# Moving the last block's query products and their copies in an attention and FFN kernel

## The chip, the cores and the metric

The kernel runs on one core of one Trainium2 chip. The metric is the device time of one execution in microseconds, and the time before is the median of three runs. TensorE multiplies, VectorE, ScalarE and GpSimd (POOL in the profile) work on its results, and SyncE (SP) issues most of the transfers.

## What is computed

64 sequences of 32 positions with 512 channels go through a conditioned mixing layer, attention with 32 heads in 8 key groups, a residual, a grouped convolution and a gated FFN with low-rank factors. The part that matters here is the attention; each sequence attends causally to its own 32 positions.

```python
q = jnp.dot(x, Wq).reshape(b, t, H, HD).transpose(0, 2, 1, 3)
kv = jnp.dot(x, Wkv).reshape(b, t, G, 2, HD).transpose(2, 3, 0, 1, 4)
...
scores = jnp.einsum('bhqd,bhkd->bhqk', q, k)
scores = jnp.where(causal[None, None], -jnp.inf, scores)
weights = jax.nn.softmax(scores * (1.0 / HD ** 0.5), axis=-1)
ctx = jnp.einsum('bhqk,bhkd->bhqd', weights, v)
...
x = x + _L0_attn_ref(_L0_cond_ref(...), Wq, Wkv, Wo, bo)
x = x + _L0_ffn_ref(_L0_cond2_ref(...), ...)
```

## The kernel before

The 2048 rows are projected in four blocks of 512 (`BLOCKS`). For each block TensorE makes the mixed input `y`, its value product, its key product and `REP` = 4 query products. A product in `project(blk, j)` (L1147) is 12 matmuls of 128x512: high parts, low parts of `y`, low parts of the weight; j = 0 is the key, j = 1 to 4 are the queries. They alternate between two PSUM banks, `front[0]` and `front[1]`, and ScalarE empties each with `copy_queries` (L728), so that a product waits for the copy of the one two before it. The last block's queries go to `q_odd`, and SyncE stores them by `store_queries` (L444) to be loaded again for the steps that need them.

Attention runs in 16 steps (`QUADS`), each of four sequences, as a software pipeline over the engines. The loop variable is n; each engine has its own loop, written out by hand, and the order in it is the order of the work:

- TensorE (L1248): scores n (L1257 the mask, L1263 the 16 products), then late query products where n is 1 or 2 (`LATE_Q` = 2, so the last two of the four), the grouping of the convolution's weights at n = 2 (L1271), the context of step n - 3 (L1285), the output projection of step n - 4 (L1299).
- VectorE (L982): transpose of scores n (L989), sum of step n - 1 (L997), maxima of step n (L980), reciprocal (L1004), transpose of the probabilities of step n - 2 (L1010), low parts of the context of step n - 3 (L1025).
- GpSimd (L641): shift of step n by its maxima (L646), normalisation of step n - 1 (L653), splits of the down factors at n = 2, 3, 4 (L660, L667), residual addition of step n - 4 (L676). Ahead of the loop it clears `v_wide`, splits the four low parts of the output weight `wo_lo` by a subtraction (L631), and clears four edges of the convolution's windows (L637, L638).
- ScalarE (L801): the late query's copy at n = 1 and 2 (L803), ahead of that step's exponential (L822); spreading of the values in even steps (L791), packing of the convolution's weights at n = 2 (L827), one copy of the down factors in each of the first five steps (L832), which waits for `down_sb`, and the high part of the context of step n - 2 (L842).
- SyncE (L513): loads of query and key groups (`queries_and_keys`, L454; group g serves steps 2g and 2g + 1), the store of the last queries at n = 3, the convolution's shift at n = 4. `down_sb` is loaded right behind the first two groups (L512).

The first two groups' loads start when the last block's key product has been copied to `k_all` (L754, L476). Four of the eight `k_wide` loads of the first group are issued by ScalarE (L769), the others by SyncE. Scores 0 wait for all of them. Scores n wait for the transpose of scores n - 2.

The high parts of the output weight (`wo_hi`, L779) are copied by ScalarE ahead of the attention loop, two behind each of the two early query copies.

Of the kernel before, what the change touches and what calls it, by code (L numbers as in the profile page):

```python
# [18 lines left out]
G, REP, HD = 8, 4, 16  # L19
# [5 lines left out]
BLOCKS = N // BLOCK  # L25
TILES = BLOCK // P
BB = BLOCK // S
BT = P // S
# [17 lines left out]
SUM = 1  # L46
# [4 lines left out]
F2_HEAD = 8  # L51
STAGES = 3
RESID_PHASES = ((), (0, 1), (2, 3), ())
LATE_Q = 2
GROUPS = S // CG
SPOTS = 2 * BT
WIN = D // SPOTS
# [3 lines left out]
def adaln_attention_ffn(nc, x, params, wq, wk, wv, wo, bo, conv, f1, f3, f2, up_factors, down_factors,  # L61
                        ident, causal, out):
    with ExitStack() as ctx:
# [46 lines left out]
        wo_loaded = sem("wo_loaded")  # L110
        wo_hi_split = sem("wo_hi_split")
        wo_lo_split = sem("wo_lo_split")
# [57 lines left out]
        near_zeroed = sem("near_zeroed")  # L170
# [34 lines left out]
        with ExitStack() as room:  # L205
            wo_hi = sb("wo_hi", [GD, REP, D], room, F32R)
# [41 lines left out]
        with ExitStack() as room:  # L248
            f2_hi_head = sb("f2_hi_head", [P, F2_HEAD, D], room, F32R)
            near_head = sb("near_head", [P, 2, BB, WIN], room)  # L250
# [39 lines left out]
        with ExitStack() as room:  # L290
            sb("room6_head", [P, DC * HID], room)
            wo_sb = sb("wo_sb", [GD, REP, D], room)
        with ExitStack() as room:
            sb("room6_head_again", [P, DC * HID], room)
            near_tail = sb("near_tail", [P, 2, BB, WIN], room)
# [39 lines left out]
        def in_windows(columns):  # L335

            return columns.rearrange("p (r w h) -> p h r w", r=BT, h=2)
# [242 lines left out]
        def _(pool):  # L580
# [33 lines left out]
            for i, phase in enumerate(RESID_PHASES):  # L614
                pool.wait_ge(y_lo_ready, (i + 1) * DC)
                for tile in [blk * TILES + t for blk in phase for t in range(TILES)]:
                    blk, t = divmod(tile, TILES)
# [8 lines left out]

            pool.wait_ge(front_filled, (BLOCKS - 1) * USES + DC + 1)
            pool.memset(v_wide[:, :, :, :, :], 0.0).then_inc(v_cleared, 1)
            for j in range(REP):
                pool.wait_ge(wo_hi_split, j + 1)  # L630
                pool.tensor_tensor(wo_lo[:, j, :].rearrange("p (h r w) -> p h r w", h=2, r=BT), in_windows(wo_sb[:, j, :]),  # L631
                                   wo_hi[:, j, :].rearrange("p (h r w) -> p h r w", h=2, r=BT).bitcast(F32),
                                   ALU.subtract).then_inc(wo_lo_split, 1)

            pool.wait_ge(wo_lo_split, REP)
            for pair in (near_head, near_tail):
                pool.memset(pair[:, :, :, 0:1], 0.0).then_inc(near_zeroed, 1)  # L637
                pool.memset(pair[:, :, :, WIN - 1:WIN], 0.0).then_inc(near_zeroed, 1)  # L638
            wide = [P, 2 * BT * REP, S]

            for n in range(QUADS + OUT):  # L641
                if due(n, 0):

                    pool.wait_ge(top_ready, n + 1)
                    pr = probs[:, n % PROBS]
                    pool.tensor_tensor(pr, pr, top[:, n % PROBS].unsqueeze(2).to_broadcast(wide), ALU.subtract)\  # L646
                        .then_inc(shifted, 1)
                if due(n, SUM):

                    m = n - SUM  # L650
                    pool.wait_ge(inv_ready, m + 1)
                    pr = probs[:, m % PROBS]
                    pool.tensor_tensor(pr, pr, inv[:, m % PROBS].unsqueeze(2).to_broadcast(wide), ALU.mult)\  # L653
                        .then_inc(probs_ready, 1)
                if n in (SUM + 1, SUM + 2):

                    own = slice((n - SUM - 1) * HID // 2, (n - SUM) * HID // 2)
                    pool.wait_ge(down_stacked, 1)
                    pool.wait_ge(probs_ready, n - SUM + 1)
                    pool.tensor_tensor(a_down_s[2 * S:3 * S, own], a_down[2 * S:3 * S, own],  # L660
                                       down_part[2 * S:3 * S, own].bitcast(F32), ALU.subtract)\
                        .then_inc(down_lo_stacked, 1)
                    pool.wait_ge(down_lo_stacked, n - SUM)
                if n == SUM + 3:
                    pool.wait_ge(down_stacked, 2)
                    pool.wait_ge(probs_ready, n - SUM + 1)
                    pool.tensor_tensor(b_down_s[S:2 * S, :], b_down[S:2 * S, :],  # L667
                                       down_part[S:2 * S, 0:D].bitcast(F32), ALU.subtract).then_inc(down_lo_stacked, 1)
                    pool.wait_ge(down_lo_stacked, 3)
                if due(n, OUT):  # L670

                    tile = n - OUT
                    t = tile % TILES
                    pool.wait_ge(front_emptied[tile % 2], emptied(PROJECTED + tile) + 1)
                    pool.wait_ge(resid_loaded[t], 16 * (tile // TILES + 1))
                    pool.tensor_tensor(rows[:, t, :], out_stage[:, tile % 2, :], rows[:, t, :], ALU.add)\  # L676
                        .then_inc(x1_ready, 1)
# [7 lines left out]
        def _(act):  # L685
# [42 lines left out]
            def copy_queries(blk, j):  # L728

                n = DC + 2 + j  # L730
                act.wait_ge(front_filled, blk * USES + n + 1)
                act.copy(q_stage[blk % 2][:, :, j, :], front[n % 2][:, :].rearrange("p (b s) -> p b s", s=S))\
                    .then_inc(front_emptied[n % 2], 1)

            for i in range(BLOCKS // 2):
                for half in range(2):
                    blk = 2 * i + half
                    for c in range(DC):

                        act.wait_ge(front_emptied[c % 2], blk * (USES // 2) + emptied(c) + 1)  # L740
                        act.copy(y_hi[:, c, :], y_t[:, c, :]).then_inc(y_hi_ready, 1)
                        if blk == 0:

                            act.wait_ge(wq_loaded, 16)
                            act.copy(wkq_hi[:, 1 + c, :, :], wq_sb[:, :, c, :]).then_inc(wkq_hi_split, 1)
                    n = DC
                    act.wait_ge(front_filled, blk * USES + n + 1)
                    act.copy(v_all[:, blk * TILES:(blk + 1) * TILES, :],
                             front[n % 2][:, :].rearrange("p (t c) -> p t c", t=TILES))\
                        .then_inc(front_emptied[n % 2], 1)  # L750
                    n = DC + 1

                    act.wait_ge(front_filled, blk * USES + n + 1)
                    act.copy(k_all[:, :, blk * 2:(blk + 1) * 2, :].rearrange("p g c s -> p c g s"),  # L754
                             front[n % 2][:, :].rearrange("p (c g s) -> p c g s", c=2, s=S))\
                        .then_inc(front_emptied[n % 2], 1)
                    if blk == 0:
                        spread_mix_act(2)
                        spread_mix_act(3)
                        copy_up_factors(0)  # L760
                    if half == 1:

                        act.wait_ge(q_stored[0], 16 * (i + 1))
                    if blk == BLOCKS - 1:

                        act.wait_ge(front_emptied[n % 2], blk * (USES // 2) + emptied(n) + 1)
                        act.wait_ge(zeros_set, 3)
                        for k in range(HEADS, G):
                            act.dma_start(k_wide[k * HD:(k + 1) * HD, 0, :, k % HEADS, :], k_all[0:HD, k, :, :])\  # L769
                                .then_inc(k_loaded[0], 16)  # L770
                    for j in range(REP - (LATE_Q if blk == BLOCKS - 1 else 0)):
                        copy_queries(blk, j)
                        if blk == 0:
                            copy_up_factors(1 + j)
                        if blk == BLOCKS - 1:

                            act.wait_ge(wo_loaded, 16)
                            for part in range(j * REP // (REP - LATE_Q), (j + 1) * REP // (REP - LATE_Q)):
                                act.copy(wo_hi[:, part, :].rearrange("p (h r w) -> p h r w", h=2, r=BT),  # L779
                                         in_windows(wo_sb[:, part, :])).then_inc(wo_hi_split, 1)  # L780

            copies = stack_copies(a_down, b_down, a_down_s, b_down_s, down_part[2 * S:3 * S, :],
                                  down_part[S:2 * S, 0:D])
# [15 lines left out]
            act.wait_ge(front_emptied[DC % 2], emptied((BLOCKS - 1) * USES + DC) + 1)  # L799
            act.wait_ge(v_cleared, 1)  # L800
            for n in range(QUADS + OUT):  # L801
                if 1 <= n <= LATE_Q:
                    copy_queries(BLOCKS - 1, REP - LATE_Q + n - 1)  # L803
                if due(n, 0) and n % 2 == 0:

                    if n >= 4:
# [13 lines left out]
                if due(n, 0):  # L820
                    act.wait_ge(shifted, n + 1)
                    act.activation(probs[:, n % PROBS], probs[:, n % PROBS], ACT.Exp, scale=SCALE)\  # L822
                        .then_inc(exp_ready, 1)
                if n == LATE_Q:

                    act.wait_ge(conv_grouped, 1)
                    act.copy(conv_sb[:, :, :, :, :], ps[7][:, 0:GROUPS * 2 * S]  # L827
                             .rearrange("p (g h q o) -> p g h q o", g=GROUPS, h=2, q=BT)).then_inc(conv_packed, 1)
# [249 lines left out]
        def _(pe):  # L1078
# [169 lines left out]
            for n in range(QUADS + OUT):  # L1248
                if due(n, 0):
# [15 lines left out]
                                           q_t[part, c, :, :].rearrange("p j s -> p (j s)"),  # L1265
                                           start=False, stop=(b == BT - 1))
                    mm.then_inc(scores_ready, 1)
                if 1 <= n <= LATE_Q:
                    project(BLOCKS - 1, REP - LATE_Q + n)
                if n == LATE_Q:  # L1270
                    group_conv()  # L1271
                if due(n, TURN + 1):
                    m = n - TURN - 1
# [179 lines left out]
```

## Time and profile before

| what | before |
|---|---|
| median of 3 runs | 592.26 us (591.83 to 592.91) |
| the profiled execution | 592.54 us, its span 590.7 us |
| TensorE busy | 578.9 us, 98% |
| VectorE, ScalarE, GpSimd busy | 237.6, 172.2, 182.3 us |
| mean granted TensorE clock | 0.991 |
| projections of the last block, then attention | scores 0 start at 101.87, scores 15 at 183.76 |

Times are microseconds from the start of the span. A timeline row says when a group starts, how long it takes, the engine, the line, the operation, output <- input, and in brackets the engine's idle time ahead of it with what ended it. A row of the chain of waits says when a piece starts, how long it lasts and what it is; the chain is followed back from the last instruction to whatever released it.

### The profile page before, as it was taken

How to read it: one execution, taken by the hardware profiler on the slowest of the kernel's cores; microseconds unless marked ns; L12 is line 12 of the kernel's file. 1: busy time of each engine (PE TensorE's matmuls, PEld its weight loads, DVE VectorE, ACT ScalarE, POOL GpSimd, SP SyncE). 2: the span in 40 equal slices, each digit the busy share in tenths (PEclk: the TensorE clock that was granted, in tenths of full speed). 3: DMA queues.
4: the chain of work that ended last, by engine and by line, in shares of the span. 5: the costliest groups of instructions: out<-in, count | busy, mean ns of one | idle time of the engine just before them, and what ended most of it. 6: DMA issues, size and time to landing. Idle time of an engine off the chain costs nothing.

```text
span 590.7 us, 8111 instructions
## 1 busy us (share of the span) xinstructions
PE 578.9 (98%) x3227; PEld 466.8 (79%) x3227; DVE 237.6 (40%) x340; ACT 172.2 (29%) x296; POOL 182.3 (31%) x132
## 2 busy tenths in 40 slices
PE   9999999799999999999999999999999999999997
PEld 6988988577777778887778888778888777888885
DVE  1434542789999851111641111244111234211112
ACT  3561224564654353332121111121111102211110
POOL 3438463699999595434200000000000000000000
PEclk9999999969999999999999999999999999999999
DMA  7975648545666774000019000007400002200001
GB/s 244 344 306 158 225 161 267 144 102 172 178 157 178 240 220 88 1 0 1 1 71 226 5 1 1 2 1 206 94 0 0 0 0 76 67 0 1 0 1 71
DMA packets 70735, 59.24 MB, mean 100 GB/s; under 512 B 45072, under 2 KB 61840, under 8 KB 69584
## 3 DMA queue, kind: packets, MB, share of 16 engines
q1 hardware_dynamic: 69840, 57.43, 32.2%
q10 hardware_dynamic: 864, 1.38, 0.6%
q8 instruction: 22, 0.36, 0.3%
q14 instruction: 9, 0.07, 0.0%
HBM read 40.94 MB, written 16.79 MB: 98 GB/s over the span
## 4 chain that ended last, share of the span: by engine, by line
PE 84%; POOL 6%; DVE 4%; ACT 2%; SPq 1%; DMA 1%; issue 1%; POOLq 0%; DVEq 0%
PE twin L1333 41%; PE twin L1354 20%; PE twin L1155 7%; POOL probs L646 4%; PE twin L1299 3%; PE twin L1175 3%; PE twin L1188 3%; PE twin L1230 3%; DVE total L997 2%; ACT probs L822 2%; DVE top L980 2%; SPq L463 1%; POOL probs L653 1%; PE twin L1118 1%; DMA down_sb<-in_down_factors 1%; PE twin L1285 1%
## 5 line engine op out<-in xcount | busy, mean ns | idle before, releaser
L1046 DVE TENSOR_TENSOR gate<-twin,gate 128x512 f32<-128x512 f32 (+1 forms) x44 | 30.4, 691 | 244.5 <-PE twin L1333 244.5
L1333 PE MATMUL twin<-c_hi,f_lo 128*128 128x512 f32 (+1 forms) x352 | 96.5, 397 | 0.0
L1333 PE MATMUL twin<-c_hi,f_hi 128*128 128x512 f32 (+1 forms) x352 | 95.4, 393 | 0.0
L1333 PE MATMUL twin<-c_lo,f_hi 128*128 128x512 f32 (+1 forms) x352 | 95.3, 393 | 0.0
L1333 PEld LDWEIGHTS twin<-c_hi,f_lo 128*128 128x128 f32 (+1 forms) x352 | 65.6, 187 | 16.1 <-POOL f_lo L682 0.4
L1333 PEld LDWEIGHTS twin<-c_hi,f_hi 128*128 128x128 f32 (+1 forms) x352 | 65.5, 186 | 15.6 <-issue 0.3
L1333 PEld LDWEIGHTS twin<-c_lo,f_hi 128*128 128x128 f32 (+1 forms) x352 | 65.5, 186 | 15.5
L868 ACT ACTIVATE gate<-twin 128x512 f32<-128x512 f32 (+1 forms) x44 | 26.3, 598 | 169.9 <-PE twin L1333 169.9
L1354 PE MATMUL twin<-f_lo,gate_hi 128*128 128x512 f32 (+1 forms) x176 | 68.6, 390 | 0.0
L871 ACT CAST gate_hi<-gate 128x512 fp32r<-128x512 f32 (+1 forms) x44 | 27.3, 622 | 126.6 <-DVE gate L1046 126.6
L1354 PE MATMUL twin<-f_hi_head,gate_hi 128*128 128x512 f32 x128 | 50.1, 392 | 0.0
L1354 PE MATMUL twin<-f_hi_head,gate_lo 128*128 128x512 f32 x128 | 49.8, 389 | 0.0
L1052 DVE TENSOR_TENSOR gate_lo<-gate,gate_hi 128x512 fp32r<-128x512 f32 (+1 forms) x44 | 30.6, 696 | 26.1 <-ACT gate_hi L871 26.1
L682 POOL TENSOR_TENSOR f_lo<-f_sb,f_hi 128x512 fp32r<-128x512 f32 (+1 forms) x22 | 28.1, 1300 | 33.6 <-ACT f_hi L860 33.6
L1354 PEld LDWEIGHTS twin<-f_lo,gate_hi 128*128 128x128 f32 (+1 forms) x176 | 33.1, 188 | 6.9
L646 POOL TENSOR_TENSOR probs<-probs,top 128x1024 f32<-128x1024 f32 x16 | 30.6, 1914 | 9.2 <-DVE top L980 9.0
L653 POOL TENSOR_TENSOR probs<-probs,inv 128x1024 f32<-128x1024 f32 x16 | 30.7, 1916 | 0.4 <-DVE inv L1004 0.4
L1354 PEld LDWEIGHTS twin<-f_hi_head,gate_hi 128*128 128x128 f32 x128 | 24.2, 189 | 6.3 <-issue 1.2
L1354 PEld LDWEIGHTS twin<-f_hi_head,gate_lo 128*128 128x128 f32 x128 | 24.0, 188 | 5.0
L1285 PE MATMUL twin<-probs_t,v_wide 128*64 128x128 f32 x256 | 19.3, 297 | 6.5 <-DVE probs_t L1010 5.5
L989 DVE STREAM_TRANSPOSE probs<-twin 128x1024 f32<-128x1024 f32 x16 | 19.6, 1224 | 11.2 <-PE twin L1263 11.2
L676 POOL TENSOR_TENSOR rows<-out_stage,rows 128x512 f32<-128x512 f32 x16 | 21.2, 1326 | 7.8 <-ACT out_stage L818 7.7
(150 smaller groups left out, 813.8 us busy)
## 6 DMA issues: line engine op xcount, KB each, us to landing
f_sb<-in_f SPq DMA_DIRECT2D x2, 2752.0 KB, 20.1
x_dram<-resid_stage SPq DMA_DIRECT2D x16, 256.0 KB, 2.1
rows<-x_dram SPq DMA_DIRECT2D x16, 256.0 KB, 3.5
q_t<-q_dram SPq DMA_DIRECT2D x8, 512.0 KB, 5.5
x_dram<-rows SPq DMA_DIRECT2D x16, 256.0 KB, 3.3
rows<-x_dram SPq DMA_DIRECT2D x8, 512.0 KB, 4.5
out<-rows SPq DMA_DIRECT2D x12, 256.0 KB, 2.0
x_sb<-in_x SPq DMA_DIRECT2D x2, 1024.0 KB, 7.6
```

What stands on the lines that cost most here:

```text
L646: pool.tensor_tensor(pr, pr, top[:, n % PROBS].unsqueeze(2).to_broadcast(wide), ALU.subtract)\
L653: pool.tensor_tensor(pr, pr, inv[:, m % PROBS].unsqueeze(2).to_broadcast(wide), ALU.mult)\
L676: pool.tensor_tensor(rows[:, t, :], out_stage[:, tile % 2, :], rows[:, t, :], ALU.add)\
L682: pool.tensor_tensor(lo, w, hi.bitcast(F32), ALU.subtract).then_inc(lo_split, 1)
L868: act.activation(gate[0:w, h % 2, :], up_bank[2 * (h % 2)][0:w, :], ACT.Silu)\
L871: act.copy(gate_hi[0:w, h % 2, :], gate[0:w, h % 2, :]).then_inc(gate_hi_ready, 1)
L1046: dve.tensor_tensor(gate[0:w, h % 2, :], up_bank[2 * (h % 2) + 1][0:w, :], gate[0:w, h % 2, :], ALU.mult).then_inc(gate_ready, 1)
L1052: dve.tensor_tensor(gate_lo[0:w, h % 2, :], gate[0:w, h % 2, :], gate_hi[0:w, h % 2, :].bitcast(F32), ALU.subtract).then_inc(gate_lo_ready, 1)
L1155: mm = pe.matmul(front[n % 2][:, :], w[:, c, :], y[:, c, :], start=(m == 0 and c == 0), stop=(m == 2 and c == DC - 1))
L1285: mm = pe.matmul(ctx_bank[m % 2][part, b * P:(b + 1) * P], v_wide[:, m * BT % BB + b, h].rearrange("p g d -> p (g d)"), probs_t[:, m % 2, ...
L1333: mm = pe.matmul(bank[0:w, :], f[:, c, :], c_part[:, c, :], start=(n == 0 and c == 0), stop=(n == 2 and c == DC - 1))
L1354: mm = pe.matmul(down_bank[t][:, :], g[0:w, h % 2, t * P:(t + 1) * P], f, start=(h == 0 and n == 0), stop=(h == HC - 1 and n == 2))
```

## The change

All four query products of the last block come behind scores: one behind scores 0, two behind scores 1, one behind scores 2. ScalarE copies each behind the exponential of the same step. The grouping and packing of the convolution's weights stay at step 2. ScalarE copies the high parts of the output weight in one go ahead of the loop. GpSimd splits two low parts ahead of the loop, two behind the first shift, and clears the four edges at step 5.

```diff
-LATE_Q = 2
+LATE_Q = 4
+LATE_STEPS = (0, 1, 1, 2)
+PACK_AT = 2
...
 # GpSimd
-            for j in range(REP):
+            def split_wo(j):
+
                 pool.wait_ge(wo_hi_split, j + 1)
                 pool.tensor_tensor(wo_lo[:, j, :].rearrange("p (h r w) -> p h r w", h=2, r=BT), in_windows(wo_sb[:, j, :]),
                                    wo_hi[:, j, :].rearrange("p (h r w) -> p h r w", h=2, r=BT).bitcast(F32),
                                    ALU.subtract).then_inc(wo_lo_split, 1)
...
+            split_wo(0)
+            split_wo(1)
...
+                if n == 0:
+                    split_wo(2)
+                    split_wo(3)
+                if n == SUM + TILES:
+
+                    pool.wait_ge(wo_lo_split, REP)
+                    for pair in (near_head, near_tail):
+                        pool.memset(pair[:, :, :, 0:1], 0.0).then_inc(near_zeroed, 1)
+                        pool.memset(pair[:, :, :, WIN - 1:WIN], 0.0).then_inc(near_zeroed, 1)
...
 # ScalarE
+                    if blk == BLOCKS - 1:
+
+                        act.wait_ge(wo_loaded, 16)
+                        for part in range(REP):
+                            act.copy(wo_hi[:, part, :].rearrange("p (h r w) -> p h r w", h=2, r=BT),
+                                     in_windows(wo_sb[:, part, :])).then_inc(wo_hi_split, 1)
                     for j in range(REP - (LATE_Q if blk == BLOCKS - 1 else 0)):
                         copy_queries(blk, j)
...
-                if 1 <= n <= LATE_Q:
-                    copy_queries(BLOCKS - 1, REP - LATE_Q + n - 1)
...
                     act.activation(probs[:, n % PROBS], probs[:, n % PROBS], ACT.Exp, scale=SCALE)\
                         .then_inc(exp_ready, 1)
-                if n == LATE_Q:
+                for k, step in enumerate(LATE_STEPS):
+                    if n == step:
+                        copy_queries(BLOCKS - 1, REP - LATE_Q + k)
+                if n == PACK_AT:
...
 # TensorE
-                if 1 <= n <= LATE_Q:
-                    project(BLOCKS - 1, REP - LATE_Q + n)
-                if n == LATE_Q:
+                for k, step in enumerate(LATE_STEPS):
+                    if n == step:
+                        project(BLOCKS - 1, REP - LATE_Q + 1 + k)
+                if n == PACK_AT:
                     group_conv()
```

## Rows read from the trace of the kernel before

**Rows 1.** The page's clock line: 40 slices, tenths of full TensorE speed.

```profile
PEclk9999999969999999999999999999999999999999
```

**Rows 2.** Chain of waits, 93 to 121 us: start, duration, what.

```profile
105.94 5.42 DMA down_sb<-in_down_factors
...
111.38 1.34 ACT down_part L832
...
112.75 0.58 ACT q_odd L732
...
113.36 1.06 ACT probs L822
...
116.87 1.91 POOL probs L646
```

**Rows 3.** Chain of waits, 119 to 141 us: GpSimd's shifts of steps 3 to 6.

```profile
122.51 1.91 POOL probs L646
...
128.18 1.92 POOL probs L646
...
134.73 1.92 POOL probs L646
...
140.19 1.93 POOL probs L646
```

**Rows 4.** Timeline of TensorE, 92 to 121 us.

```profile
101.87 0.51 PE L1257 MATMUL twin<-mask,mask_rows 64*128 64x512 f32 x2 [0.52 <-DMA k_wide<-k_all]
...
102.99 0.48 PE L1257 MATMUL twin<-mask,mask_rows 64*128 64x512 f32 x1
...
104.33 1.19 PE L1155 MATMUL twin<-y_hi,wkq_hi 128*128 128x512 f32 x4
...
107.31 0.51 PE L1257 MATMUL twin<-mask,mask_rows 64*128 64x512 f32 x2
...
118.30 1.98 PE L1285 MATMUL twin<-probs_t,v_wide 128*64 128x128 f32 x16 [4.49 <-DVE probs_t L1010]
```

**Rows 5.** Timeline of all engines, 84 to 105 us.

```profile
95.94 0.58 ACT L754 COPY k_all<-twin 128x512 f32<-128x512 f32 x1 [2.16 <-PE twin L1155]
...
96.94 2.68 SPq L463 DMA_DIRECT2D k_wide<-k_all  x4
```

**Rows 6.** Timeline of VectorE, 101 to 122 us.

```profile
103.40 1.25 DVE L989 STREAM_TRANSPOSE probs<-twin 128x1024 f32<-128x1024 f32 x1 [10.13 <-PE twin L1263]
104.69 1.22 DVE L980 TENSOR_REDUCE top<-probs 128x32 f32<-128x1024 f32 x1
...
114.44 1.22 DVE L997 TENSOR_REDUCE total<-probs 128x32 f32<-128x1024 f32 x1 [2.71 <-ACT probs L822]
```

**Rows 7.** Stretches: bounds, length, TensorE busy (instructions), granted clock, DMA share, GB/s.

```profile
113.50:114.00 0.50, 0.31 (x6) 1.00 0.00 0
...
117.00:117.50 0.50, 0.00 (x0) 0.74 0.71 295
...
123.50:124.00 0.50, 0.24 (x2) 0.50 0.20 33
...
127.00:127.50 0.50, 0.50 (x2) 0.52 0.00 0
```

**Rows 8.** Timeline of SyncE's queue, 95 to 125 us.

```profile
115.74 0.33 SPq L451 DMA_DIRECT2D q_dram<-q_odd  x1
...
117.01 5.95 SPq L463 DMA_DIRECT2D k_wide<-k_all  x8
```

**Rows 9.** Instructions of L463, the loads of `k_wide`, 95 to 125 us.

```profile
DMA to landing us min/median/max: 1.9/2.7/5.3
```

**Rows 10.** Instructions of L451, the four stores of queries.

```profile
DMA to landing us min/median/max: 4.0/4.7/8.6
```

**Rows 11.** Timeline of GpSimd, 95 to 142 us.

```profile
100.54 5.11 POOL L631 TENSOR_TENSOR wo_lo<-wo_sb,wo_hi 128x512 fp32r<-128x512 f32 x4 [5.44 <-ACT wo_hi L779]
...
140.19 1.92 POOL L646 TENSOR_TENSOR probs<-probs,top 128x1024 f32<-128x1024 f32 x1 [0.42 <-DVE top L980]
```

More of the change, by code:

```diff
@@ L633, in _ @@
                                    ALU.subtract).then_inc(wo_lo_split, 1)
[L635 to L638, printed above, removed]
             wide = [P, 2 * BT * REP, S]
+            split_wo(0)
+            split_wo(1)
             for n in range(QUADS + OUT):
@@ L774, in _ @@
                             copy_up_factors(1 + j)
[L775 to L780, printed above, removed]
             copies = stack_copies(a_down, b_down, a_down_s, b_down_s, down_part[2 * S:3 * S, :],
```

## The prediction

> **What bounds the kernel now.** I read the page's clock line first: one of its 40 slices is at 0.6, the others at 0.9 or more [rows 1]. It lies where the kernel passes from projections to attention, which is where the change works. Then I read the chain of waits through that place, to see what starts attention's own rhythm.
>
> The chain [rows 2] says: SyncE issues the load of `down_sb` at 105.94, it lands at 111.36, ScalarE copies it (1.34), copies one late query (0.58), and only then takes the exponential of step 1 at 113.36. VectorE's sum and step 2's row maxima follow, and GpSimd shifts step 2's scores at 116.87. From there GpSimd carries the chain: the shift of step 3 starts 5.64 later (122.51), those of steps 4 and 5 another 5.67 and 6.55 later, because beside shift and normalisation GpSimd splits parts of the down factor; step 6 follows 5.46 later, and so do the others: the round trip shift, exponential, sum, maxima [rows 3]. No load stands in this chain after 116.87. So whatever moves the start of step 2's shift moves the end of the kernel by the same amount. That start is the number to forecast.
>
> The TensorE timeline [rows 4] shows the other side: key projection, two query projections, a 0.52 us wait for `k_wide`, scores 0 at 101.87, scores 1 at 102.99, a query product, scores 2 at 107.31, a query product, and then, after scores 3, an idle stretch of 4.49 us until 118.30. TensorE has room there; in the chain it isn't present.
>
> **Part 1: two more query products behind the scores.** Removed ahead of scores 0: two products, 24 matmuls. The key product ends near 95.9 (ScalarE's copy of its result starts at 95.94). But scores 0 can't start then: they wait for eight 16 KB `k_wide` loads, half of them issued on ScalarE's queue behind that copy, half on SyncE's from 96.94 for 2.68, so until 99.62, and are released at 101.87 [rows 4, 5]. Those loads hang on the key product and its copy, which are untouched. So the start of scores 0 stays at 101.87, and the removed 5.5 us of work only turns into idle time: gain 0. The bound on that gain is 0 to 2.25 us (a landing the moment the last issue ends); I take 0, as the released row is measured.
>
> Added behind it: new order scores 0, Q0, scores 1, Q1, Q2, scores 2, Q3, grouping of the convolution, scores 3. From 101.87 to the start of scores 2, by start-to-start distances [rows 4]: scores 0 1.12 (101.87 to 102.99), one product 2.98 (104.33 to 107.31), scores 1 1.34 (102.99 to 104.33), two more products 2 x 2.98 = 11.40. Scores 2 start at 113.27, where before they started at 107.31. VectorE's transpose of scores 0 began 1.53 after their start [rows 4, 6], so transpose 2 begins at 114.80. Before, it was long done: VectorE stood 2.71 us waiting for exponential 1 ahead of sum 1 at 114.44. That cover is used up. Its order there is transpose 2, sum 1, maxima 2: 1.29 from a transpose to what follows (103.40 to 104.69), then 2.43 from sum 1 to shift 2 (114.44 to 116.87) [rows 2, 6]. Shift 2 starts at 114.80 + 1.29 + 2.43 = 118.52, against 116.87: **+1.65**.
>
> Is anything else later than that? Maxima 0 come as before. Scores 1 now follow Q0: they start at 105.97, their transpose at 107.5, their maxima end near 110.0. Shift 1 (1.9) ends near 112, well ahead of transpose 2. So at full clock TensorE's order of work is the last thing to arrive.
>
> **Part 2: the clock.** TensorE now stands still from about 95.9 to 101.87, 5.9 us. The trace shows a similar stop: work ended at 113.81, and the granted clock fell from full (2.4 GHz) to half (1.2 GHz) at 117.24 (0.74 granted in the half microsecond from 117.0) [rows 7]. That is a stop of 4.49 us; a stop of 5.9 should fall too. Then it worked 118.30 to 122.7 and from 123.76 on, at half clock, and rose at 127.49. There it cost nothing, since GpSimd carried the chain. Now it would hit exactly the stretch in which TensorE is last. The price is half of the slow working time, since at a granted 0.50 [rows 7] the array does half its work. Bounds for the slow working time: 3.73 (from 123.76, work without a gap, to 127.49) and 9.19 (from 118.30). Both ends give losses of 1.87 and 4.60. The new stretch has no gaps, so it is near the lower one, but starts from a longer stop; I take 4.7 us, a loss of **2.35**. If the clock doesn't fall the loss is 0. Meanwhile shift 1 is later too, but by the delay of scores 1, which is at most the same loss.
>
> The Trainium skill, page "TensorE: Matmul & The Clock Gate", section "Part 1: The HAM clock gate", says the monitor doesn't start anew with a kernel, so the same kernel shows different counts of slow matmuls from run to run. By it the sum would lie anywhere between the held clock (593.9) and the long slow stretch (598.5), not at one value; the trace, a single execution, can't show that.
>
> **Part 3: copies behind each exponential.** Four copies of 0.58 as before, only placed later; the 0.58 ahead of exponential 1 goes (gain 0 to 0.61, the distance 112.75 to 113.36). I take 0: exponential 1 would be done at 113.8, before transpose 2 ends at 116.0. Q2's product needs Q0's copy (same bank) and Q3's needs Q1's: those copies come after exponential 0 (about 110) and exponential 1 (about 114 to 116), each in time for the product behind it. Nothing is queued wrongly on ScalarE: behind Q3's copy stand the convolution's packing and the first context copy, needed from step 4 on.
>
> SyncE queues matter more. The store of the last queries waits for Q3's copy; it moves from 115.74 to about 124.5 (exponential 2 would end near 123.9, four microseconds later than before, and a copy takes 0.6). Behind it lie the loads of group 3, whose issue ran from 117.01 for 5.95, so now to about 131.7 [rows 8]; with the longest landing of 5.3 [rows 9] they are in by 137.0. Scores 6 are wanted near 134.7 + 4.0 = 138.7. ScalarE waits for that store before it stages the first output tile; its longest landing is 8.6 [rows 10]: 133.1, while exponential 4 behind it waits for shift 4, which started at 128.18 and ended 1.9 later, now at 134.1. Cost 0 each, with 0.6 to 1.6 us of margin.
>
> **Part 4: the output weight's low parts.** The same four subtractions as before (5.11 us together [rows 11]). Before they ended just as maxima 0 came in. Now two run before the first shift and two behind it, about 108 to 111, while shift 1 can't start before maxima 1 (110.0, later with a slow clock). Cost 0 to 0.6; I take 0. The four little clears go to step 5, where GpSimd idled 0.42 ahead of 140.19 [rows 11]; their 0.3 fits. Without that cover: +0.3. The round trip and FFN are unchanged.
>
> **The sum.** +1.65 + 2.35 = +4.00 on the profiled execution's own 592.54 (span 590.7 and 1.84 around it) = 596.54. That execution is 0.28 over the median 592.26, so for the median 596.3.
>
> **Rivals.**
> - Clock holds: the idle stretch doesn't bring the clock down, or not in the median run. Then only the order costs: 592.26 + 1.65 = 593.9. For: full clock persisted for 3.4 us of standstill. Against: this stop is 1.4 us longer than the one that fell.
> - Long slow stretch: 9.2 us of slow work as after 118.30: 592.26 + 1.65 + 4.60 = 598.5.
> - Faster: ScalarE's start of the rhythm comes earlier. Place: exponential 1. The loads of group 2, issued right behind `down_sb`, now wait for scores 1, so `down_sb` may land in 4.0 us (the fastest of the query stores [rows 10], which are larger) instead of 5.42: -1.42, and the query copy no longer stands ahead: -0.61. Together 592.26 - 2.03 = 590.2. It decides only if transpose 2 comes early: any gain at all needs it before 113.15, 1.65 us before my 114.80, and a gain of 1.2 us needs it before 111.95. For that scores 0 would have to start at 99.0, while their loads are still being issued.
> - The change does nothing that reaches the end: VectorE and GpSimd take up the delay, for example because the standing work in steps 3 to 5 was held by slow scores 5 in the old trace. 592.3 to 592.9. Against: GpSimd is without a gap there.
>
> **How the numbers follow.** Measurement tells about 0.2%, 1.2 us, from no change. Forecast with a fallen clock, 595 to 598: 0.62. Clock holds: 0.18 (a third of it inside 0.2%, should shorter matmul groups trim the order's cost). Long slow stretch or a queue's margin gone: 0.06. No effect: 0.06. Faster: 0.08. So slower 0.80, same 0.12, faster 0.08. The time is that of the likeliest, 596.3. The range 593.3 to 598.3 leaves out faster, no effect and the tail.
>
> **What would show it.** TensorE idle 95.9 to 101.9 with scores 0 still at 101.9; granted clock 0.5 in the stretch behind; scores 2 at 114 to 117; VectorE's sum 1 waiting for nothing from ScalarE; shift 2 at 120 to 122; steps of 5.6, 5.7, 6.5, 5.46 after it as before. Wrong if scores 0 start earlier than 101, if the clock stays full, or if shift 2 comes before 118.

## The result and the profile after

The changed kernel takes 595.94 us (median of six runs, 595.49 to 596.73), the kernel before 592.42 (six runs). The ratio is 1.0057, with a 95% interval of 1.0047 to 1.0067: slower by 0.6%, 0.36 us under the forecast. The profiled execution is one of 595.73 us with a span of 593.9, 3.2 more than before.

The clock line of the page now has two lower slices, where it had one [rows 1]:

```profile
PEclk9999998979999999999999999999999999999999
...
PE 87%; DVE 6%; POOL 3%; ACT 2%; DMA 1%; issue 1%; SPq 0%; ACTq 0%; DVEq 0%
```

One, at 0.8, lies where the projections end, the other, at 0.7, in the first steps of attention. The second line is the page's chain by engine: GpSimd's share of it went from 6% to 3%, TensorE's from 84% to 87%, VectorE's from 4% to 6%. The chain of waits through the place (start, duration, what) shows how:

```profile
98.48 2.56 DMA k_wide<-k_all
...
101.17 0.80 PE twin L1268 x2
...
103.67 3.60 PE twin L1166 x12
...
108.60 5.65 PE twin L1166 x24
...
115.62 1.25 DVE probs L1000
...
119.18 1.92 POOL probs L647
...
126.07 1.98 PE twin L1297 x16
128.04 4.94 PE twin L1311 x12
...
134.36 1.25 DVE probs L1000
...
137.92 1.93 POOL probs L647
...
143.38 1.92 POOL probs L647
```

Where the old chain ran over the load of `down_sb` and ScalarE [rows 2], it now runs over the key loads and then over TensorE alone, up to the transpose of scores 2 (115.62). Shift 2 starts at 119.18 instead of 116.87, 2.31 later. The second half of the piece is one I had not foreseen: TensorE is in the chain again from 126.07, at 1.98 and 4.94 us for a context and an output projection, and shift 5 (137.92) stands 7.46 behind shift 4 (130.46), where the old distance was 6.55 [rows 3].

The whole change in time has happened by shift 8. Its rows before and after, from GpSimd's timeline:

```profile
151.12 1.92 POOL L646 TENSOR_TENSOR probs<-probs,top 128x1024 f32<-128x1024 f32 x1 [0.43 <-DVE top L980]
```

```profile
154.31 1.92 POOL L647 TENSOR_TENSOR probs<-probs,top 128x1024 f32<-128x1024 f32 x1 [0.43 <-DVE top L991]
```

From it to the end of the span pass 439.58 us before and 439.59 after.

TensorE's timeline, to hold against [rows 4]:

```profile
101.17 0.80 PE L1268 MATMUL twin<-mask,mask_rows 64*128 64x512 f32 x2 [5.80 <-DMA k_wide<-k_all]
...
103.60 1.82 PE L1166 MATMUL twin<-y_hi,wkq_hi 128*128 128x512 f32 x4
...
107.20 0.50 PE L1268 MATMUL twin<-mask,mask_rows 64*128 64x512 f32 x2
...
114.17 0.51 PE L1268 MATMUL twin<-mask,mask_rows 64*128 64x512 f32 x2
...
126.07 1.98 PE L1297 MATMUL twin<-probs_t,v_wide 128*64 128x128 f32 x16 [3.04 <-DVE probs_t L1021]
```

The engine stands still for 5.80 us, scores 0 start no earlier relative to the key product, and scores 2 start at 114.17, where they started at 107.31. The stretches say when the clock changed (bounds, length, TensorE busy, granted clock, DMA share, GB/s):

```profile
98.00:98.50 0.50, 0.00 (x0) 0.67 0.95 385
104.50:105.00 0.50, 0.50 (x2) 0.50 0.11 19
105.00:105.50 0.50, 0.50 (x4) 1.00 0.10 15
125.00:125.50 0.50, 0.00 (x0) 0.97 1.19 262
132.00:132.50 0.50, 0.50 (x3) 0.70 0.29 107
```

It fell to half near 98.2, rose at 105.0, fell again near 125.5, rose near 132.3. Both times it fell while TensorE stood still.

### The profile page after: what moved, and what is told of

It reads as the page before. It is cut to its first block, busy times and chain, and to the rows that moved or that the text cites. A ratio compares the mean times of both kernels' runs of the same rounds, so it can differ in the third digit from the quotient of the medians.

```text
span 593.9 us, 8111 instructions
## 1 busy us (share of the span) xinstructions
PE 579.5 (98%) x3227; PEld 466.7 (79%) x3227; DVE 237.6 (40%) x340; ACT 171.8 (29%) x296; POOL 182.2 (31%) x132
## 4 chain that ended last, share of the span: by engine, by line
PE 87%; DVE 6%; POOL 3%; ACT 2%; DMA 1%; issue 1%; SPq 0%; ACTq 0%; DVEq 0%
PE twin L1345 41%; PE twin L1366 20%; PE twin L1166 9%; PE twin L1311 4%; POOL probs L647 3%; PE twin L1186 3%; PE twin L1199 3%; PE twin L1241 3%; DVE total L1008 2%; DVE top L991 2%; ACT probs L830 2%; PE twin L1297 1%; PE twin L1274 1%; PE twin L1155 1%; PE twin L1129 1%
## 5 line engine op out<-in xcount | busy, mean ns | idle before, releaser
L830 ACT ACTIVATE probs<-probs 128x1024 f32<-128x1024 f32 x16 | 16.9, 1059 | 27.5 <-POOL probs L647 27.5
```

## The experiments

Unless said otherwise the changed kernel is the base. "Behind the key copy" means from the start of ScalarE's copy to `k_all`, the event that starts the key loads; it takes out the half microsecond by which the projections ahead differ from execution to execution (95.94 before, 95.41 in the profile above).

**The changed kernel again.** 

> The changed kernel once more, on the chip of the three kernels beside it. Every theory: 595.9, ratio to before 1.0057; TensorE's clock falls in the stop ahead of scores 0. If the clock falls in the second stop (3.0 us ahead of the context of step 1) only in some executions, the profile may show shift 5 either 6.55 or 7.5 us behind shift 4.

Measured: 596.48 us, ratio 1.0068 (1.0055 to 1.0081). Its stretches:

```profile
99.50:100.00 0.50, 0.00 (x0) 0.97 1.00 165
106.50:107.00 0.50, 0.50 (x3) 0.70 1.15 151
127.00:127.50 0.50, 0.17 (x2) 0.78 1.05 213
130.50:131.00 0.50, 0.50 (x3) 0.81 0.20 32
```

The same stop (6.09 us here), but the clock fell at 100.0 and rose at 106.8. Slow work from scores 0 (101.92) was 4.9 us, against 3.8 in the first profile. The second slow stretch was short (it ended near 130.7), and shift 5 stood 6.55 behind shift 4 (131.72 to 138.27): the old distance, nothing lost. The Trainium skill, page "TensorE: Matmul & The Clock Gate", section "Part 1: The HAM clock gate", says that the same kernel shows different counts of slow matmuls from run to run. These two profiles agree: 3.8 and 4.9 us of slow work behind the same stop.

The mean granted clock of the timed executions says how common each case is. Of the eleven executions of the changed kernel (six above, five here) five have 0.987 to 0.989, as the first profile (0.988), and six have 0.991, as the second. They took 596.3 and 596.2 us on average: the longer second stretch doesn't show in the median.

**TensorE kept busy in the first stop.**

```diff
             pe.wait_ge(mask_made, 3)
+            keep_clock(22)
```

> 22 matmuls of 512 columns that nobody reads fill the 5.8 us stop ahead of scores 0, so that the clock is at full speed there. Clock theory: scores 0 still start near 101.2, scores 0 take 1.1 instead of 2.4 and the product behind them 3.0 instead of 3.6, shift 2 starts 1.9 us earlier, total 1.9 us less: 594.0, ratio 1.0025. Order-only theory (the clock costs nothing at the end, the whole 3.5 us are TensorE's order): unchanged, 595.9.

Measured: 593.43 us (12 runs), ratio 1.0016 (1.0005 to 1.0027). TensorE's timeline:

```profile
95.50 5.15 PE L1094 MATMUL twin<-mask_rows 128*128 128x512 f32 x22
101.82 0.50 PE L1269 MATMUL twin<-mask,mask_rows 64*128 64x512 f32 x2 [1.16 <-DMA k_wide<-k_all]
...
103.14 1.20 PE L1166 MATMUL twin<-y_hi,wkq_hi 128*128 128x512 f32 x4
...
106.08 0.50 PE L1269 MATMUL twin<-mask,mask_rows 64*128 64x512 f32 x2
...
113.06 0.51 PE L1269 MATMUL twin<-mask,mask_rows 64*128 64x512 f32 x2
```

Twenty-two matmuls more, and 3 us less than the changed kernel beside it. Scores 0 take 1.32 (101.82 to 103.14) instead of 2.43, the product behind them 2.94 instead of 3.60. Shift 2 starts at 118.06:

```profile
118.06 1.92 POOL L647 TENSOR_TENSOR probs<-probs,top 128x1024 f32<-128x1024 f32 x1 [3.89 <-DVE top L991]
...
129.37 1.91 POOL L647 TENSOR_TENSOR probs<-probs,top 128x1024 f32<-128x1024 f32 x1
135.91 1.91 POOL L647 TENSOR_TENSOR probs<-probs,top 128x1024 f32<-128x1024 f32 x1
```

That is 16.24 behind scores 0. It was 15.00 before (101.87 to 116.87), 18.01 in the first profile of the changed kernel and 18.51 in the second. So TensorE's order costs 1.24 us and the slow clock 1.8 to 2.3 at this point. The order-only theory falls; the total fell by 3.05 where I had expected 1.9. The spans of the two profiled executions differ by 2.4 (594.3 and 591.9), of which 2.27 are there at shift 2; this kernel's profile has no second slow stretch (shift 4 to 5: 6.54). Its timed executions are less even: ten of the twelve have a granted clock of 0.993 to 0.997, against 0.999 in the profile, so TensorE was slow in them at places that this profile doesn't show. They were not the longer ones (593.5 us on average, the other two 593.9). Where the rest of the 3.05 comes from stays open.

**Both stops filled.**

```diff
                         pe.wait_ge(conv_packed, 1)
+                        keep_clock(10)
```

> As the kernel with the first stop filled, and 10 more unread matmuls in the stop ahead of the context of step 1. Clock theory: the output projection of step 0 runs at full clock (2.9 us instead of 4.9), scores 5 no longer hold VectorE, shift 5 starts 6.55 behind shift 4 instead of 7.46; 0.9 less again: 593.1, ratio 1.0011. What is left over before (0.7 to 1.1 us) is the order of TensorE's work. Theory that the second slow stretch is hidden: 594.0.

Measured: 594.39 us, ratio 1.0031 (1.0019 to 1.0043). A miss: not below the kernel with one stop filled, whose interval it overlaps. In the profile (span 591.3) the clock is full throughout, shift 2 is 16.27 behind scores 0 and shift 5 is 6.53 behind shift 4, as in the one before. Since that one had no second slow stretch in its profile, the 0.9 us couldn't be gained there; what makes the timed executions of this kernel slower than its own profile (593.14 us) stays open. It isn't the clock, which was 0.998 to 1.0 in all six.

**The third query product behind scores 2.**

```diff
-LATE_STEPS = (0, 1, 1, 2)
+LATE_STEPS = (0, 1, 2, 2)
```

> The changed kernel with the third query product behind scores 2 instead of ahead of them (steps 0, 1, 2, 2). Order theory: scores 2 start 2.8 us earlier, transpose 2 is done near 114.0, just as exponential 1 is; shift 2 starts near 116.6 instead of 119.2, total 2.5 us less: 593.4, ratio 1.0015. If the delay came from the clock or from GpSimd alone, the place of that product would not matter: 595.9.

Measured: 595.30 us, ratio 1.0048 (1.0030 to 1.0065): 1.2 less than the kernel beside it, not 2.5. GpSimd's shifts 2, 3 and 4, and VectorE's transposes 2 and 3:

```profile
117.37 1.92 POOL L647 TENSOR_TENSOR probs<-probs,top 128x1024 f32<-128x1024 f32 x1 [1.67 <-DVE top L991]
124.97 1.91 POOL L647 TENSOR_TENSOR probs<-probs,top 128x1024 f32<-128x1024 f32 x1 [2.01 <-DVE top L991]
130.63 1.92 POOL L647 TENSOR_TENSOR probs<-probs,top 128x1024 f32<-128x1024 f32 x1
```

```profile
113.57 1.25 DVE L1000 STREAM_TRANSPOSE probs<-twin 128x1024 f32<-128x1024 f32 x1 [0.24 <-PE twin L1274]
121.35 1.25 DVE L1000 STREAM_TRANSPOSE probs<-twin 128x1024 f32<-128x1024 f32 x1 [2.69 <-PE twin L1274]
```

The gain was there at shift 2 (15.82 behind scores 0 instead of 18.51), as expected. One step later most of it was given back: scores 3 now stood behind two products, transpose 3 waited 2.69 us for them, and shift 3 came 7.60 behind shift 2 instead of 5.63. Of 2.69 us 0.72 are left at shift 3. The product's place matters, but neither of the two places tried is free. My estimate had stopped at the next shift.

The execution profiled here took 596.60 us, 1.3 above the median, and lost time at another place, far behind attention, where TensorE waits for GpSimd's first low part of the FFN's factors:

```profile
215.07 1.20 PE L1345 MATMUL twin<-c_hi,f_lo 128*128 128x512 f32 x4 [1.53 <-POOL f_lo L692]
```

The second profile of the changed kernel has no such wait. From shift 8 to the end of the span pass 439.5 to 439.8 us in every profile here but two: this one with 441.2, and 440.3 in the kernel with the same edit below. So a median can also differ by a wait that lies outside the head of attention.

**GpSimd's work in the old order.** The four subtractions and the four clears go back ahead of the loop.

```diff
             split_wo(0)
             split_wo(1)
+            split_wo(2)
+            split_wo(3)
...
-                if n == 0:
-                    split_wo(2)
-                    split_wo(3)
```

> The changed kernel with GpSimd's work in its old order: all four subtractions of the output weight and the four clears ahead of the attention loop. My theory: GpSimd idled 4.3 us ahead of shift 0 in the changed kernel, and shift 1 waits for VectorE's maxima, so nothing changes: 595.9, ratio 1.0057. Rival: the two subtractions behind shift 0 hold shift 1, and taking them away gives 0.4 us: 595.5.

Measured: 595.70 us, ratio 1.0050 (1.0035 to 1.0065), with an interval that overlaps those of the changed kernel. In this kernel shift 1 waits 2.92 us for its maxima, in the changed one it still waited 0.39. That part of the change costs and brings nothing here. In its profile shift 2 is 18.00 behind scores 0, as in the first profile of the changed kernel.

**Only the copies behind the exponentials.** The base is the kernel before.

```diff
-                if 1 <= n <= LATE_Q:
-                    copy_queries(BLOCKS - 1, REP - LATE_Q + n - 1)
...
                         .then_inc(exp_ready, 1)
+                if 1 <= n <= LATE_Q:
+                    copy_queries(BLOCKS - 1, REP - LATE_Q + n - 1)
```

> The kernel before, with only the two late query copies moved behind the exponentials of their steps. Chain theory: exponential 1 starts 0.61 earlier, all behind it too: 591.8, ratio 0.9990. Rival: the copy ahead of it was covered by the load of down_sb in any case: 592.4.

Measured: 591.96 us (12 runs; 592.62 for the kernel before beside them), ratio 0.9990 (0.9980 to 0.9999). The interval all but reaches 1, so the median alone would be weak evidence; in the profile shift 2 is 14.49 behind scores 0, before it was 15.00. About the 0.6 us expected are there, and the chain of [rows 2] was read rightly. So the change holds one useful part, small as it is, which the later products cover up.

**And the down copies one step later.** The base is the kernel of the last experiment.

```diff
-                if n < len(copies):
+                if 1 <= n <= len(copies):
...
-                    act.copy(*copies[n]).then_inc(down_stacked, 1)
+                    act.copy(*copies[n - 1]).then_inc(down_stacked, 1)
```

> The kernel before, with the copies behind the exponentials and the five copies of the down factors one step later, so that exponential 1 no longer waits for the load of down_sb. Chain theory: exponential 1 follows shift 1 at 110.4 instead of 113.4, VectorE's transpose 2 (done at 111.8) becomes the last to arrive, shift 2 starts near 114.2 instead of 116.9, 2.6 less: 589.8, ratio 0.9956. Rival: the head of attention is hidden further on and the end doesn't move: 592.4.

Measured: 589.62 us, ratio 0.9946 (0.9929 to 0.9964), faster than the kernel before and than the one of the last experiment (591.96). Its chain of waits:

```profile
110.07 1.10 DVE probs L989
111.18 1.10 DVE total L997
...
113.48 1.92 POOL probs L646
...
120.37 1.98 PE twin L1285 x16
122.35 4.87 PE twin L1299 x12
...
132.14 1.93 POOL probs L646
```

The load of `down_sb` has left the chain. Shift 2 is 12.21 behind scores 0 (101.27) instead of 15.00. Some of it is given back: TensorE stands still for 3.04 us, works at half clock (4.87 for twelve matmuls), and shift 5 is 7.37 behind shift 4.

**The same edit in the changed kernel.** 

> The changed kernel with ScalarE's five copies of the down factors one step later, the edit that took 2.4 us off the kernel before when it came on top of the later query copies. Theory that TensorE's order is last in the changed kernel: exponential 1 is not what transpose 2 and sum 1 wait for (VectorE stood 2.96 us waiting for scores 2), so nothing changes: 596.2, ratio 1.006. Rival, ScalarE still starts the rhythm: 2 us less, 594.

Measured: 595.68 us, ratio 1.0050 (1.0034 to 1.0066): what takes 2.3 us off the kernel before does nothing here. VectorE waited 2.96 us for scores 2 ahead of transpose 2, shift 2 was 18.30 behind scores 0. So it is TensorE's scores 2, late by its order and by the slow clock, and not ScalarE or `down_sb`, that arrive last in the changed kernel.

**Key loads of the first group left out.**

```diff
-                for k in range(G if g else HEADS):
+                for k in range(G if g else 0):
...
-                        for k in range(HEADS, G):
+                        for k in range(HEADS, HEADS + 2):
```

> The changed kernel with six of the eight loads that bring the first group's keys left out (its first steps so attend over zero keys in six of eight key groups), and the waits for them lowered. Theory that scores 0 start when those loads land and that TensorE's work from there on reaches the end: the last issue ends near 98 instead of 99.3, the query load of 512 KB beside them (landing 3.7 to 6.2) becomes the bound, scores 0 start 4.0 to 5.2 behind the copy of the key product instead of 5.8 to 6.0, and the total falls by as much, about 1: 595.2. Rival: scores 0 are held by the query load in any case: no change, 596.2.

Measured: 595.76 us, ratio 1.0056 (1.0037 to 1.0074). This kernel leaves part of the computation out, so only its times are of use. Scores 0 started at 101.72, 6.12 behind the key copy: no earlier, as the rival had it. But the chain of waits doesn't name the query load as the rival did; it names one of the two key loads, which took 4.56 us to land. And the edit changed a second thing: with SyncE's four key loads gone, the second group's 512 KB of queries were issued right behind the first group's. The next run takes the first group's queries away from there.

**And the first group's queries loaded early.** The base is the kernel of the last experiment.

```diff
+                    sp.wait_ge(q_stored[0], 16 * BLOCKS // 2)
+                    load_group_queries(0)
                     sp.wait_ge(front_emptied[1], i * (USES // 2) + emptied(DC + 1) + 1)
-                    sp.wait_ge(q_stored[0], 16 * BLOCKS // 2)
```

> The kernel with six of the eight key loads of the first group left out (same part of the computation missing), and the first group's queries loaded ahead of the wait for the key product, from about 91 us. Theory that the 512 KB query load was last for scores 0 once the key loads were few: now only two key loads hold them, scores 0 start near 100 instead of 101.7 (4.3 behind the key copy instead of 6.1), total 1.5 less: 594.3. Rival, two key loads alone take until 101.7 to land beside the second group's query load: scores 0 unchanged, 595.8.

Measured: 595.36 us, ratio 1.0048 (1.0035 to 1.0062). Scores 0 started 5.52 behind the key copy. Two loads of 16 KB took this long, by the chain of waits:

```profile
96.63 0.73 ACTq L786
...
97.39 3.96 DMA k_wide<-k_all
101.35 0.14 issue
101.49 0.79 PE twin L1275 x2
```

The first group's queries, issued at 91.55 and landed by 98.8 at the latest, don't hold scores 0 here. In this kernel the second group's 512 KB of queries were still issued together with the two key loads; the last run of this section issues them later.

**The fastest kernel with TensorE busy in its stop.** Base: the kernel with the later down copies, and the ten unread matmuls at the same place as above.

> The fastest kernel so far (the kernel before, query copies behind the exponentials, down copies one step later), with 10 unread matmuls in TensorE's stop of 3.0 us ahead of the context of step 1. Clock theory: the output projection of step 0 takes 2.9 instead of 4.9 us, scores 5 no longer hold VectorE, shift 5 starts 6.55 instead of 7.4 behind shift 4: 0.8 less, 588.8, ratio 0.9940. Rival: the timed executions don't have that slow stretch, or it is hidden: 589.6.

Measured: 589.13 us (588.59 to 589.80), ratio 0.9939 (0.9924 to 0.9953). The profile shows the mechanism: shift 4 at 124.95, shift 5 at 131.48, 6.53 apart instead of 7.37. The gain in the median, 0.5 against the kernel without the filler, lies inside the intervals, so it is shown in the profile only. This is the fastest kernel of the study.

**The fastest kernel with queries early and GpSimd in the changed order.** 

> The fastest kernel so far with its first group's queries loaded ahead of the wait for the key product, all eight key loads kept, and GpSimd's order of the changed kernel (two low parts of the output weight behind shift 0, the clears at step 5). Theory: the key loads see less traffic and land 0.5 to 1 us earlier, and shift 0 can follow, since GpSimd is free from 102.6: 588.4. Rival: key loads land as before, 5.8 to 6 us behind the key copy: 589.1.

Measured: 590.31 us, ratio 0.9962 (0.9948 to 0.9975), 1.2 slower than the last. The intervals of the two just touch (the last one's ends at 0.9953), but the profiles agree: from the key copy to shift 8 pass 53.78 us here and 52.80 there. Scores 0 did start earlier: at 100.36 they followed the early products without waiting, 5.33 behind the key copy, with all eight key loads landed. The first group's queries were out of the way here, issued at 90.81, and the second group's came only at 98.37, behind SyncE's four key loads. The last key load was issued by 98.63 and all had landed 1.7 us later; before the change scores 0 were released 2.25 us behind the last issue (99.62 to 101.87). In the two kernels with fewer key loads the 512 KB loads were issued alongside, and a key load took 3.96 us beside one of them and 4.56 beside two. Which transfers hinder which was not measured further. The loss is on GpSimd:

```profile
104.49 1.92 POOL L651 TENSOR_TENSOR probs<-probs,top 128x1024 f32<-128x1024 f32 x1 [2.03 <-DVE top L993]
106.37 2.58 POOL L638 TENSOR_TENSOR wo_lo<-wo_sb,wo_hi 128x512 fp32r<-128x512 f32 x2
108.90 1.92 POOL L651 TENSOR_TENSOR probs<-probs,top 128x1024 f32<-128x1024 f32 x1
114.36 1.91 POOL L651 TENSOR_TENSOR probs<-probs,top 128x1024 f32<-128x1024 f32 x1 [1.67 <-DVE top L993]
```

The two subtractions stand between shift 0 and shift 1 and hold shift 1 to 4.41 behind shift 0, where the last kernel had 2.40. In the changed kernel they were free, because scores 1 came late. A smaller loss beside it: TensorE stood still for 3.14 us already ahead of the context of step 0, where nothing fills the stop, its clock fell to half near 115.1, and shift 5 came 6.73 behind shift 4 instead of 6.53.

## Why the prediction was right

The number (596.3 against 595.94), the sign and the place were right. The forecast is a rise of 4.00 us, the medians rose by 3.52. Its condition "clock holds" (593.9) was tried too: 593.43 and 594.39 with the stop filled. Term by term, against the two profiles of the changed kernel and the one with the stop filled:

- **Start of scores 0, gain 0**: right. 5.76 and 6.05 us behind the key copy, 5.93 before. 24 matmuls taken out ahead became 5.80 us of standstill.
- **TensorE's order, +1.65**: the mechanism was right, the size too large: 1.24 at full clock. Two products in a row take 5.65 without the gap that stands at the end of one alone (I had 2 x 2.98), and sum 1 begins 1.18 behind transpose 2 instead of 1.29; against that, scores 0 with a product behind them take 1.32 and not 1.12.
- **Clock, +2.35**: 1.77 and 2.27, with 3.8 and 4.9 us of slow work, where I took 4.7. The choice near the lower bound was right, and so was the range: it isn't one number but varies with the execution. The low slice of the old clock line was placed wrongly: at 118 to 133 us it is not the passage from projections to attention but attention's first steps. The fall and the rise themselves were read rightly from [rows 7].
- **Missed: the second stop.** I read step 4's output projection as unchanged. In the changed kernel TensorE waits 3.04 us for the probabilities of step 1, and in both profiles the clock fell in that stop. In the first it stayed low until 132.3 and shift 5 came 0.91 late; in the second it rose at 130.7 and nothing was lost. The kernel before had its slow stretch over the same output projection without loss in its profile, since there scores 5 were nearly in time (VectorE waited 1.06 us, and GpSimd was still at work until the shift). The rival of no effect named just this point and had the sign of it wrong.
- **"There it cost nothing"** holds for the one profiled execution of the kernel before. Among those timed beside the experiments the ten with a granted clock of 0.996 took 592.1 us on average and the 24 with 0.991, the profile's own, 592.9. No trace shows what makes these 0.9 us.
- **The sum of the first profile**: projections ahead -0.53, loads -0.17, order +1.24, clock +1.77, second stretch +0.91 make +3.22; the span grew by 3.2. At shift 2, the number to forecast, that is +2.31 where I had +4.00, and 119.18 lies just under the 120 to 122 that I had named as the sign; the second profile has 120.43. Two terms were too large by 1.0 together, and a missed one of 0.9 filled the gap, so the closeness of the total is partly luck. For the second profile the same sum is -0.07, +0.12, +1.24 and +2.27, with nothing for the second stretch: +3.56, and the span grew by 3.6. There the clock term was right by itself and only the order was too large.
- **Copies behind the exponentials, 0**: worth 0.6 without the late products, as put. That they bring nothing in this kernel follows from VectorE's wait of 2.96 us for scores 2; no run puts them back ahead of the exponentials here.
- **Low parts, 0**: right (GpSimd's old order changes nothing), but only because of the cover named; without it they hold shift 1.
- **SyncE's queues, 0**: right. The store came at 122.73 (forecast 124.5), the loads of group 3 from 124.01, and no engine waited for either.
- **The faster rival** fell as argued: `down_sb` was no longer waited for to speak of (0.24 us), and it landed 5.2 us after its issue, not 4.0; but transpose 2 was late.

## What to carry to other kernels

Work moved out of the way of a step that waits for a load gains nothing, and behind that step it is work in front of everything that follows. Before moving work, ask what the step waits for, and follow the delay over the next two or three steps, not only the next. The idle time left behind has a price of its own when TensorE's clock falls in it, and that price is paid where the engine has just become the bound. Here the cheap gain was elsewhere on the old chain: a copy that waited for a load ahead of the first exponentials, moved by one step.

## What was not expected of the hardware

Unread matmuls made the kernel faster: 22 of them in a stop of 5.8 us took it from 596.48 to 593.43 in the same session. The slow stretch behind the same stop differed by 1.1 us between two executions of the same program, and a second stop of 3.04 us led to a loss of 0.91 in one and none in the other. A 16 KB load took 3.96 us to land with one load of 512 KB issued alongside and 4.56 with two.
